# A gated cross-attention and expert block: the query and output projections as three split products

## The reference

```
def xattn(q, k, v, mask, w_q, b_q, w_k, b_k, w_v, b_v, w_o, b_o):
    qh, kh, vh = heads(q @ w_q + b_q), heads(k @ w_k + b_k), heads(v @ w_v + b_v)
    scores = einsum('bhqd,bhkd->bhqk', qh, kh) * D_HEAD ** (-0.5)
    scores = where(mask == 0, -10000.0, scores)
    out = einsum('bhqk,bhkd->bhqd', softmax(scores), vh)
    return merge_heads(out) @ w_o + b_o

x = x + tanh(g_xattn) * xattn(layernorm(x), ctx, ctx, mask, ...)
x = x + tanh(g_ffn) * ffn(layernorm(x))     # shared expert + top 2 of 4 experts, 688 wide
```

## Time and profile before

| | us |
|---|---|
| median of 3 runs (1084.17 to 1085.97) | 1085.26 |
| the profiled execution's own time | 1084.47 |
| its span, first to last instruction | 1082.6 |
| PE busy in the span | 971.2 (90%) |
| DVE busy | 561.7 (52%) |
| ACT busy | 498.8 (46%) |
| POOL busy | 471.4 (44%) |
| mean granted TensorE clock | 0.955 |

### The profile page before, as it was taken

The page is one execution under the profiler, slowest core; times in us unless marked ns, Lnnn a source line. Parts: engine busy times, 40 slices in busy tenths (PEclk is TensorE's granted clock), DMA queues, the critical chain, the costliest instruction groups (busy, mean ns, idle before and its releaser), DMA issues. The chain is left out here.

```text
span 1082.6 us, 21517 instructions
## 1 busy us (share of the span) xinstructions
PE 971.2 (90%) x6399; PEld 870.2 (80%) x6400; DVE 561.7 (52%) x1255; ACT 498.8 (46%) x1806; POOL 471.4 (44%) x641
## 2 busy tenths in 40 slices
PE   5678999999999999999747599999999999999995
PEld 3457888888888888888636489999999999999995
DVE  4555555556565565643389544444444444444442
ACT  3777676677776767663122222222222222222221
POOL 4345445545554444333107434444444444444442
PEclk9789999999999999999956699999999999999999
DMA  5100102100111110000053112222222222222221
GB/s 175 34 18 14 34 3 57 33 19 26 36 33 33 33 33 21 11 30 21 21 181 105 51 25 39 39 39 39 39 40 40 40 39 39 39 40 37 44 39 20
DMA packets 47646, 44.92 MB, mean 41 GB/s; under 512 B 14618, under 2 KB 44159, under 8 KB 47583
## 3 DMA queue, kind: packets, MB, share of 16 engines
q0 software_dynamic: 12864, 17.57, 10.0%
q1 hardware_dynamic: 33655, 26.37, 8.1%
q10 hardware_dynamic: 1064, 0.21, 0.1%
HBM read 26.39 MB, written 17.43 MB: 40 GB/s over the span
## 5 line engine op out<-in xcount | busy, mean ns | idle before, releaser
L1482 POOL DMA_INDIRECT out_rows<-yout,add_at x67 | 107.2, 1600 | 200.7 <-DVE yout L1540 200.7
L480 ACT ACTIVATE prob<-p_s,negmax 128x77 f32<-128x77 f32 x512 | 160.7, 349 | 40.1 <-DVE negmax L681 38.7
L1549 DVE TENSOR_TENSOR hid<-p_gu,sil 128x688 f32<-128x688 f32 x67 | 58.6, 875 | 168.9 <-ACT sil L1517 168.9
L1517 ACT ACTIVATE sil<-p_gu 128x688 f32<-128x688 f32 x67 | 50.0, 747 | 197.0 <-PE p_gu L1583 197.0
L480 ACT ACTIVATION_READ_ACCUMULATOR prob<-p_s,negmax 128x1 f32 x512 | 118.0, 231 | 0.0
L928 PE MATMUL p_f<-xnT_hi,swgu_hi 128*128 128x256 f32 x384 | 116.0, 302 | 1.0 <-DVE shid L698 0.9
L1583 PE MATMUL p_gu<-wgu_hi,fxT_hi 128*128 x402 | 112.6, 388 | 1.0 <-DVE fxT_lo L1534 1.0
L928 PE MATMUL p_f<-xnT_hi,swgu_lo 128*128 128x256 f32 x384 | 108.4, 282 | 0.0
L928 PE MATMUL p_f<-xnT_lo,swgu_hi 128*128 128x256 f32 x384 | 108.4, 282 | 0.0
L1583 PE MATMUL p_gu<-wgu_hi,fxT_lo 128*128 x402 | 106.7, 373 | 0.0
L1583 PE MATMUL p_gu<-wgu_lo,fxT_hi 128*128 x402 | 106.6, 374 | 0.0
(11 more groups left out here) (234 smaller groups left out, 2467.5 us busy)
## 6 DMA issues: line engine op xcount, KB each, us to landing
xr<-in_x SPq DMA_DIRECT2D x16, 256.0 KB, 3.1
xn_scratch<-xn SPq DMA_DIRECT2D x16, 256.0 KB, 2.1
out_rows<-syout SPq DMA_DIRECT2D x16, 256.0 KB, 2.2
raw<-in_L_ffn_ed SPq DMA_DIRECT2D x4, 688.0 KB, 4.2
raw<-in_L_ffn_eg SPq DMA_DIRECT2D x4, 640.0 KB, 4.1
raw<-in_L_ffn_eu SPq DMA_DIRECT2D x4, 640.0 KB, 4.1
mask_in<-in_mask_Bx1xSxS_if SPq DMA_DIRECT2D x16, 77.0 KB, 2.6
xin<-xn_scratch,get_at POOLq DMA_INDIRECT x67, 2.7
```

Of the source, the lines that this page charges most:

```text
L480: last = act.activation(prob[n % 2][t][:, m * PW + h * SK:m * PW + (h + 1) * SK], p_s[:, 2 * t + h // 4, col:col + SK], ACT.Exp, bias=negm ...
L1482: pool.indirect_dma_start(out, bass.IndirectOffsetOnAxis(add_at[k][:, :], 0), yout[k][:, :], None, compute_op=ALU.add).then_inc(s_add, 16)
L1517: act.activation(sil[:, :], p_gu[:, 0:FF], ACT.Silu).then_inc(s_sil, 1)
L1549: nc.vector.tensor_tensor(hid[:, 0:FF], p_gu[:, FF:2 * FF], sil[:, :], ALU.mult).then_inc(s_hid, 1)
```

## The change

The operands of both projections are split like those of the other products. The weights are loaded to `wraw` (views of the output buffer `yout`, idle at the start) and split once: ACT makes `wq_hi` and `wo_hi`, DVE `wq_lo` and `wo_lo`. Per unit, ACT's two copies out of `p_m` now write the high parts `xT[0]` and `oT[0]`, and two new DVE instructions, `xT_lo` and `o_lo`, subtract them from `p_m`. `q_T` and `out_proj` wait for the low parts and run 12 split matmuls where 8 plain instructions stood. `wk` and `wv` move into the buffers `th` and `ah`.

```diff
-        wq = sb("wq", [P, KC, H])
-        wo = sb("wo", [P, KC, H])
+        wq = [sb(f"wq_{s}", [P, KC, H], f32r) for s in ("hi", "lo")]
+        wo = [sb(f"wo_{s}", [P, KC, H], f32r) for s in ("hi", "lo")]
...
+        wk, wv = th, ah
+        wraw = {"q": yout[:, 0, :, :], "o": yout[:, 1, :, :]}
...   ACT: xT_copy and o_copy
-                act.activation(xT[:, :, :], cols(p_m[:, :]), ACT.Copy).then_inc(s_xTc, 1)
+                act.activation(xT[0][:, :, :], cols(p_m[:, :]), ACT.Copy).then_inc(s_xThi, 1)
...
-                act.activation(oT[:, :, :], cols(p_m[:, :]), ACT.Copy).then_inc(s_oT, 1)
+                act.activation(oT[0][:, :, :], cols(p_m[:, :]), ACT.Copy).then_inc(s_oThi, 1)
...   ACT: start-up
             normed(0)
+            act.wait_ge(s_wq, 16)
+            act.activation(wq[0][:, :, :], wraw["q"], ACT.Copy).then_inc(s_wqhi, 1)
...
             normed(1)
+            act.wait_ge(s_wo, 16)
+            act.activation(wo[0][:, :, :], wraw["o"], ACT.Copy).then_inc(s_wohi, 1)
...   DVE: new functions
+            def xT_lo(n):
+                dve.wait_ge(s_xThi, n + 1)
+                wait(dve, s_q, n)
+                nc.vector.tensor_tensor(xT[1][:, :, :], cols(p_m[:, :]), xT[0][:, :, :], ALU.subtract).then_inc(s_xTlo, 1)
+
+            def o_lo(n):
+                dve.wait_ge(s_oThi, n + 1)
+                wait(dve, s_Wo, n)
+                nc.vector.tensor_tensor(oT[1][:, :, :], cols(p_m[:, :]), oT[0][:, :, :], ALU.subtract).then_inc(s_oTlo, 1)
...   DVE: start-up
             nc.vector.tensor_tensor(kTs[1][:, :, :], kT[:, :, :], kTs[0][:, :, :], ALU.subtract).then_inc(s_klo, 1)
+            dve.wait_ge(s_wqhi, 1)
+            nc.vector.tensor_tensor(wq[1][:, :, :], wraw["q"], wq[0][:, :, :], ALU.subtract).then_inc(s_wqlo, 1)
+            xT_lo(0)
...
+            dve.wait_ge(s_wohi, 1)
+            nc.vector.tensor_tensor(wo[1][:, :, :], wraw["o"], wo[0][:, :, :], ALU.subtract).then_inc(s_wolo, 1)
...   DVE: step(i)
+                if has(i - 2):
+                    o_lo(i - 2)
                 if has(i):
                     half_max(i, 0)
...
                 for w in weights_in(i)[0:2]:
                     w_lo(w)
+                if has(i + 1):
+                    xT_lo(i + 1)
                 if has(i - 3):
                     inner(i - 3, 1)
...   PE
             def q_T(n):
-                pe.wait_ge(s_xTc, n + 1)
+                pe.wait_ge(s_xTlo, n + 1)
+                pe.wait_ge(s_wqlo, 1)
...
+                        for q, (w, x) in enumerate(PASSES):
+                            last = nc.tensor.matmul(p_m[:, m * UT * P:(m + 1) * UT * P], wq[w][:, k, m * P:(m + 1) * P],
+                                                    xT[x][:, k, :], start=(k == 0 and q == 0),
+                                                    stop=(k == KC - 1 and q == 2))
...
             def out_proj(n):
-                pe.wait_ge(s_oT, n + 1)
+                pe.wait_ge(s_oTlo, n + 1)
...
+                        for q, (x, w) in enumerate(PASSES):
+                            last = nc.tensor.matmul(p_m[:, t * H:(t + 1) * H], oT[x][:, m, t * P:(t + 1) * P],
+                                                    wo[w][:, m, :], start=(m == 0 and q == 0),
+                                                    stop=(m == KC - 1 and q == 2))
```

More of the change, by code:

```diff
@@ L123, in attend_and_share @@
         ctxT = sb("ctxT", [P, KC, B * SK])
-        wk = sb("wk", [P, KC, H])
-        wv = sb("wv", [P, KC, H])
-        wq = sb("wq", [P, KC, H])
-        wo = sb("wo", [P, KC, H])
+        wq = [sb(f"wq_{s}", [P, KC, H], f32r) for s in ("hi", "lo")]
+        wo = [sb(f"wo_{s}", [P, KC, H], f32r) for s in ("hi", "lo")]
         gw_sb = sb("gw_sb", [E, H])
@@ L144, in attend_and_share @@
         xh = sb("xh", [P, UT, H])
-        xT = sb("xT", [P, KC, UT * P])
+        xT = [sb(f"xT_{s}", [P, KC, UT * P], f32r) for s in ("hi", "lo")]
         qT = [sb(f"qT_{s}", [P, 2, KC, UT * P], f32r) for s in ("hi", "lo")]
@@ L154, in attend_and_share @@
         pT = sb("pT", [P, KC * CH, UT * P])
-        oT = sb("oT", [P, KC, UT * P])
+        oT = [sb(f"oT_{s}", [P, KC, UT * P], f32r) for s in ("hi", "lo")]
         half = sb("half", [P, UT])
@@ L269, in _ @@
             load_x(0)
-            sp.dma_start(wq[:, :, :], v["w_q"].rearrange("(c p) d -> p c d", p=P)).then_inc(s_wq, 16)
+            sp.dma_start(wraw["q"], v["w_q"].rearrange("(c p) d -> p c d", p=P)).then_inc(s_wq, 16)
             load_mask(0)
@@ L281, in _ @@
                 sp.dma_start(raw[kind][0:FT, (FC - 1) * H:FC * H], src[full:FF, :]).then_inc(s_raw[kind], 16)
-            sp.dma_start(wo[:, :, :], v["w_o"].rearrange("(c p) d -> p c d", p=P)).then_inc(s_wo, 16)
+            sp.dma_start(wraw["o"], v["w_o"].rearrange("(c p) d -> p c d", p=P)).then_inc(s_wo, 16)
             for n in range(2, XR):
@@ L831, in q_T @@
             def q_T(n):
-                pe.wait_ge(s_xTc, n + 1)
+                pe.wait_ge(s_xTlo, n + 1)
+                pe.wait_ge(s_wqlo, 1)
                 for m in range(KC):
                     for k in range(KC):
-                        last = nc.tensor.matmul(p_m[:, m * UT * P:(m + 1) * UT * P], wq[:, k, m * P:(m + 1) * P],
-                                                xT[:, k, :], start=(k == 0), stop=(k == KC - 1))
+                        for q, (w, x) in enumerate(PASSES):
+                            last = nc.tensor.matmul(p_m[:, m * UT * P:(m + 1) * UT * P], wq[w][:, k, m * P:(m + 1) * P],
+                                                    xT[x][:, k, :], start=(k == 0 and q == 0),
+                                                    stop=(k == KC - 1 and q == 2))
                 last.then_inc(s_q, 1)
@@ L883, in out_proj @@
             def out_proj(n):
-                pe.wait_ge(s_oT, n + 1)
+                pe.wait_ge(s_oTlo, n + 1)
                 if n == 0:
-                    pe.wait_ge(s_wo, 16)
+                    pe.wait_ge(s_wolo, 1)
                 for t in range(UT):
                     for m in range(KC):
-                        last = nc.tensor.matmul(p_m[:, t * H:(t + 1) * H], oT[:, m, t * P:(t + 1) * P], wo[:, m, :],
-                                                start=(m == 0), stop=(m == KC - 1))
+                        for q, (x, w) in enumerate(PASSES):
+                            last = nc.tensor.matmul(p_m[:, t * H:(t + 1) * H], oT[x][:, m, t * P:(t + 1) * P],
+                                                    wo[w][:, m, :], start=(m == 0 and q == 0),
+                                                    stop=(m == KC - 1 and q == 2))
                 last.then_inc(s_Wo, 1)
@@ L990, in _ @@
             x_T(0)
-            pe.wait_ge(s_wq, 16)
             q_T(0)
```

12 lines of the change are left out of this document (6 added, 6 removed).

## The result

The changed kernel takes 1089.87 us (median of 5 runs, 1088.29 to 1091.07), against 1084.96 (1084.17 to 1085.97) for the kernel before in the same comparison. The ratio is 1.0045, with an interval of 1.0031 to 1.0060: slower by 4.9 us, where 3.55 were forecast. The profiled execution took 1088.29 us, the fastest of the five, with a span of 1086.6, 4.0 us more span than before.

The account below looks back on a forecast made before the run. PE bounds full steps, except ACT and DVE between gate_up(0) and xn_T; a chain between engines bounds 24.90 to 41.50 us. Lost 4.65 + 1.35 + 1.05, won 3.5: +3.55, median 1088.8 us; own range 1087.3 to 1090.3, wider 1084.6 to 1092.4.

Parts of the forecast that it names:

- rival D: Start-up: the low clock lasts 4 us of PE work longer on the chain, costing 2 us: 1090.8; chance 0.20.
- Start-up ahead of wo_lo: Subtractions wq_lo and xT_lo(0) delay q_T(0), its 12 matmuls give back 0.4 us, POOL adds 0.2: +1.25 us.
- wo_lo: Start-up: first half_max waits for wo_lo, which waits for wo_hi behind xh; +4.65 us, with 1.25 from earlier included.
- Step 0: xT_lo(1), queued behind two weight groups' splits, starts q_T(1) 2.2 us late; split matmuls return 0.85: +1.35 us.
- Step 1: Late xT_lo and shorter q_T taken as closer to each other; set at 0, bounds -0.5 and +0.5 us.
- Steps 2 and 3: No down between scores and out_proj, so the 0.53 us by which o_lo delays half_max is uncovered: +1.05 us for both.
- Full steps: out_proj 0.29 us shorter where PE is the bound, 12 steps, 3.5 us off; nothing counted for q_T.
- The wait ahead of xn_T: Full steps: PE's wait for qT_lo grows from 1.41 to 1.6 to 1.7 us, so q_T's saving counts nothing.
- Two of the signs given: In the changed profile: q_T(1) 6 to 7 us later than 27.71, step 9 beginning 5 to 6 later than 265.96.
- Rival A: out_proj saves a quarter of its 1.73 us, 0.43 in each of 12 steps: 1087.1; chance 0.14.
- Rival B: Not slower: both products' savings count in every step, 1084.7; chance 0.12.
- Rival C: xT_lo misses its DVE gap and delays the chain to qT_lo by 0.62 us in steps 3 to 14: 1096.2; chance 0.04.

Follow-up runs that it names:

- The fillers on PE: Changed kernel with eight transposes of the identity, read by nobody, on PE between x_T(0) and q_T(0); ratio 1.0025, median 1087.78 us.
- the version with the queries' product plain: Changed kernel with q_T plain, out_proj split only from unit 2, wo split at the end of step 1; ratio 0.9972 to the kernel before, median 1082.08 us.

## Why the prediction was right

The kernel became slower, for the reason given: bare waits in the start-up outweigh 12 shorter full steps. The size was less well met: 4.9 us, where the forecast had 3.55 and rival D 5.55, so by the number alone the result lies nearer to D. The term that was mis-sized is the start-up ahead of wo_lo, and what it lacked is D's cost.

- **Start-up ahead of wo_lo: +1.25 us forecast, +3.24 measured.** wq_lo and xT_lo(0) put q_T(0) at 14.98 us (15.2 forecast, and 0.2 for POOL), 1.23 later than before. But I let the twelve matmuls give back 0.4 us at the full clock; they ran at 1.2 GHz and cost 1.05 more, and the v projection, which was not in the sum, 0.96 more. The fillers on PE took 2.3 us of it away. This is rival D's mechanism, at an earlier place than where I had looked for it. I had given D a chance of 0.20 as a case by itself, with 2 us; it is rather a term that belonged into the sum. PE's idle time ahead of q_T(0) grew from 1.17 us to 2.56. All seven profiled executions with a wait of 2.5 us or more there show the low clock behind it; of the seven with 1.0 to 1.64 us, the one with fillers among them, only one does (the version with the queries' product plain, 1.01 us). So the low clock goes with the longer wait nearly always, not always.
- **wo_lo: 3.4 us forecast, 3.0 measured.** The wait is as forecast. I had stretched wo_lo to 1.1 us for the work of POOL beside it; it took 0.69, as long as alone. The ratio of 1.6 between kblk_hi and kT_lo did not carry over: POOL's instruction beside it, which began 0.02 us after it, was the longer one (1.78 us, for 1.25 to 1.47 in the kernel before).
- **Step 0: +1.35 us forecast.** q_T(1) and its wait for xT_lo went from 27.71 to 36.21, and its end from 31.42 to 39.06: with the 6.3 us of the exponentials taken off, that is +1.34. Its 12 split matmuls took 2.85 us at the low clock, for 2.86 forecast. Moving xT_lo ahead gave 0.97 us back.
- **Step 1: 0 forecast, 0 measured, in part by luck.** Step 2 began 7.64 us late: 6.3 + 1.34 and nothing more. But the other order in steps 0 and 1 gave 1.4 us back by then, 0.4 more than at q_T(1), and steps 0 and 1 run at a clock that changes between executions.
- **Steps 2 and 3: +1.05 us forecast, +0.94 measured** (24.45 for 23.99, and 26.50 for 26.02), with PE waiting 0.80 us for oT_lo in step 2.
- **Full steps: 0.29 us each forecast, 0.27 to 0.30 measured,** steps 5 and 9 unchanged; one pass in place of three took off 0.94 us for 8 matmuls of 0.12 and gave nothing in steps 5 and 9. Only out_proj counts: with the queries' product alone split a step is 29.69 us, and thinning q_T lengthened the wait by as much as it took away.
- **The wait ahead of xn_T: 1.6 to 1.7 us forecast, 1.52 measured.** xT_lo starts q_T a little later, so of the 0.29 us some 0.1 is left there. It changes nothing in the sum.

With the measured sizes: 6.3 + 1.34 + 0.94 - 3.6 = +5.0 us, for the +4.9 of the medians. The forecast had 7.05 - 3.5. The sizes come from the two profiled executions, whose spans differ by 4.0 only; the 1.0 us that came back behind the first stage is in no term. Two of the signs given were off with the start-up: q_T(1) came 8.5 us late (6 to 7 forecast), and step 9 began 7.4 us late (5 to 6). And the bounds named for the forecast's range give 1087.85 as its lower end, not 1087.3.

Rival A (a quarter off each product) is out: the split matmuls of out_proj are as far apart as those in front, 0.12 us, and a step won 0.27 us and not 0.43. The Trainium skill (FP8 and Floating Point Precision, TensorE Precision Notes) counts four passes for true fp32; by it the ratio of split to plain is 0.75, and here it is 1.44 to 1.73, 0.83. Rival B is out: PE's wait ahead of xn_T stayed, wo_lo's wait was bare, and the queries' product alone won nothing in a full step. Rival C is out: xT_lo fits, with 0.45 us to spare.

## What to carry to other kernels

A product that is cheaper on its engine gains only in the stretches where that engine is the bound; the preparation of its operands is paid first in the start-up, where nothing covers it, and a one-time weight split belongs where both of its engines have idle time in front of a need. Before counting matmuls at the full clock in a start-up, look at how long PE now stands still just ahead of them: here 1.4 us more of a wait cost another 2.3 in matmuls at 1.2 GHz. And a wait that is harmless on the chain can still be harmful to the clock: work taken out of a covered stretch here cost 13 us until PE had something else to do there.
